# A graph network's node update moved from a stage of its own into the edge steps

## The reference

```python
x = x + gnn(layernorm(x), node_vec1, src, dst, edge_attr_4, edge_attr_8, ...)
x = x + ffn(layernorm(x), ...)
```

```python
hid = silu(edge_length_embedded @ fc_w0 / sqrt(8)); w = hid @ fc_w1 / 8
y0 = segment_sum(mid0, dst); y1 = segment_sum(mid1, dst)     # products of w, h[src] and the factors
out0 = c_s * s0 + c_x * (y0 @ W_lin2_0 * z / ...)            # s0, h0: x0 @ W_sc0, x0 @ W_lin1_0
```

## Time and profile before

| | us |
|---|---|
| median of three runs (lowest, highest) | 1195.45 (1194.55, 1196.22) |
| the profiled execution's own time | 1192.31 |
| its span in the trace | 1190.3 |
| first gather to last gather | 60.6 to 554.1 |
| first routed product to last add issued | 804.3 to 1184.2 |

### The profile page before, as it was taken

The page is one execution under the profiler, slowest core; times in us unless marked ns, Lnnn a source line. Parts: engine busy times, 40 slices in busy tenths (PEclk is TensorE's granted clock), DMA queues, the critical chain, the costliest instruction groups (busy, mean ns, idle before and its releaser), DMA issues. The chain is left out here.

```text
span 1190.3 us, 30949 instructions
## 1 busy us (share of the span) xinstructions
PE 1043.2 (88%) x8929; PEld 915.6 (77%) x8929; DVE 750.4 (63%) x1842; ACT 727.2 (61%) x2353; POOL 633.0 (53%) x645
## 2 busy tenths in 40 slices
PE   3788988889998988887688999988999999999991
PEld 2567777777777777776565999988999999899991
DVE  6566677766666667775476764445666656657561
ACT  3778888888888888886355645544444443444430
POOL 4077777777777777774000044442455455455552
PEclk9979999999999999999898999998999999999996
DMA  5233333343333433434554522323243444433221
GB/s 161 94 111 109 109 111 109 109 111 108 110 110 107 111 108 109 110 108 147 161 178 177 177 90 89 102 81 118 49 111 81 85 107 112 86 74 77 41 50 22
DMA packets 91911, 125.57 MB, mean 105 GB/s; under 512 B 29278, under 2 KB 70670, under 8 KB 91712
## 3 DMA queue, kind: packets, MB, share of 16 engines
q0 software_dynamic: 31792, 67.29, 22.9%
q1 hardware_dynamic: 56128, 54.01, 14.6%
q10 hardware_dynamic: 3920, 3.41, 0.8%
HBM read 98.30 MB, written 26.36 MB: 105 GB/s over the span
## 5 line engine op out<-in xcount | busy, mean ns | idle before, releaser
L568 ACT ACTIVATE hots<-hot,sh_st 128x64 f32<-128x64 f32 x1568 | 384.9, 334 | 0.2 <-issue 0.2
L711 PE MATMUL psY<-prod,hots 128*64 128x128 f32 x2352 | 279.4, 276 | 0.0
L707 PE MATMUL psY<-prod,hots 128*64 128x256 f32 x784 | 220.6, 401 | 52.1 <-DVE prod L615 52.1
L711 PEld LDWEIGHTS psY<-prod,hots 128*64 128x64 f32 x2352 | 256.0, 138 | 0.0
L543 POOL DMA_INDIRECT x_wlo<-h_tab,src_sb x224 | 214.2, 956 | 70.1 <-issue 70.1
L1738 ACT ACTIVATE q_hf<-q_psA,x_b 128x256 f32<-128x256 f32 x232 | 110.0, 474 | 191.9 <-PE q_psA L1282 186.5
L1683 POOL DMA_INDIRECT out_rows<-q_ob,q_index x58 | 119.9, 2068 | 136.1 <-DMA out_rows<-q_ob,q_index 89.2
L543 POOL DMA_INDIRECT rows<-h_tab,src_sb x168 | 161.0, 958 | 51.2 <-issue 51.2
L707 PEld LDWEIGHTS psY<-prod,hots 128*64 128x64 f32 x784 | 83.2, 136 | 91.0 <-DVE prod L615 89.4
L1282 PE MATMUL q_psA<-q_xhi,x_whi 128*128 x464 | 132.4, 285 | 9.4 <-DVE q_xlo L1776 9.0
L1869 PE MATMUL q_psB<-x_whi,q_hhi 128*128 128x256 f32 x464 | 133.0, 287 | 0.1
(11 more groups left out here) (212 smaller groups left out, 2281.2 us busy)
## 6 DMA issues: line engine op xcount, KB each, us to landing
x_raw<-in_w SPq DMA_DIRECT2D x18, 1024.0 KB, 5.8
x_wlo<-h_tab,src_sb POOLq DMA_INDIRECT x224
x_sb<-in_x SPq DMA_DIRECT2D x5, 640.0 KB, 5.4
h_tab<-x_sb ACTq DMA_DIRECT2D x5, 640.0 KB, 3.2
u_x<-in_x SPq DMA_DIRECT2D x5, 640.0 KB, 7.0
xnew_d<-u_x SPq DMA_DIRECT2D x5, 640.0 KB, 3.5
xn_d<-u_xn SPq DMA_DIRECT2D x5, 640.0 KB, 5.1
s_xnew<-xnew_d SPq DMA_DIRECT2D x5, 640.0 KB, 5.5
```

Of the source, the lines that this page charges most:

```text
L568: ins = nc.scalar.activation(hots[p][:, c, n, :], hot[p][:, c, :], ACT.Copy, scale=sh_st[p][:, 4 * c + n:4 * c + n + 1])
L707: nc.tensor.matmul(psY[p][0:SPAN, 0:FEAT], hots[p][:, c, 0, :], prod[p][:, c, 0:4, :].rearrange("p a u -> p (a u)"), start=(c == 0), stop= ...
L711: ins = nc.tensor.matmul(side[:, k::3 - k, :][:, 0:2, :], hots[p][:, c, k + 1, :], prod[p][:, c, 4::k + 1, :][:, 0:2, :], start=(c == 0 an ...
```

## The change

1. The gathers wait once a step, at gather 0, and only for the products that free their row buffer, and gather_turn is incremented once a step. There are four row buffers, all inside x_wlo.
2. update_block is gone. Its work on a pair of tiles is spread over the eight steps of an edge iteration: with k the iteration, the pair k-1 is turned and mixed and the pair k-2 is normed, turned, scored and stored. After the last step pairs 11 and the single tile 24 remain. psE and psW are single now, so radial(j) waits for the products of step j-1. The root is made on DVE by twelve chained steps on two columns (a guess by integer shift and three Newton steps) in place of ACT's square root. The scores come out as 128 x 8, so that they need no second turn.
3. The sums y and x + s are fetched by SP for each pair (fetch_y). x + s is added in node_block by POOL (base_of) and stored to HBM (base_d); h goes through a ring of its own. The spherical factors are loaded once, for all steps; the eight edge numbers are loaded for four steps at a time. A third condition is added to R: another pass if a step begins below the tiles that are already updated.
4. The shared expert's weights are loaded at the end of node_block, the high half is split by ACT in the edge steps, the low half by DVE after the last one. All five groups of columns go through HBM, and group 0 is loaded at the end of the edge block. xnew stays in the graph's order of columns, so that the shared part's add into ob is done in two instructions. The slot sends of POOL follow other points of the shared part.
5. In the routed part POOL issues the gather of a later tile between add(d, 0) and its landing, and waits for add(d, 1) to land right behind it. For the last expert, PE does all down products of the tile before first (apart), and DVE's output comes a tile sooner (early, late).

The core of the diff:

```diff
-    RING = 7
+    RING = 4
...
-        psE = [pb(f"psE{i}") for i in range(2)]
-        psW = [ctx.enter_context(nc.psum_tensor(f"psW{i}", [P, C, 4, MUL], F32)) for i in range(2)]
+        psE = pb("psE")
+        psW = ctx.enter_context(nc.psum_tensor("psW", [P, C, 4, MUL], F32))
...
                     for c in range(C):
                         if c == 0:
-                            pool.wait_ge(prod_done, (r * T + t) * 2 + 2)
-                        if c == 1 and t >= RING - 2:
-                            pool.wait_ge(hot_done, r * T + t - RING + 3)
-                        if c == 2:
-                            pool.wait_ge(prod_done, (r * T + t) * 2 + 3)
-                        pool.sem_inc(gather_turn, 1)
+                            pool.wait_ge(prod_done, (r * T + max(t, RING - 1)) * 2 + 2)
+                        if c == 0:
+                            pool.sem_inc(gather_turn, 1)
...
+            def base_of(g):
+                for j in range(GROUP):
+                    t = g * GROUP + j
+                    pool.wait_ge(s_ready, t + 1 + 2)
...
+                    pool.tensor_tensor(s_row[:, 0:MUL], s_row[:, 0:MUL], x_row[:, 0:MUL], ALU.add)
+                    pool.tensor_tensor(s_row[:, MUL:].rearrange("p (c u) -> p c u", c=3),
+                                       s_row[:, MUL:].rearrange("p (c u) -> p c u", c=3),
+                                       x_row[:, MUL:].rearrange("p (u c) -> p c u", c=3), ALU.add).then_inc(based, 1)
```

The order on PE, and DVE's programme of a step with the burst that the root belongs to:

```diff
+            def turn_of(r, k, q, done=None, at_work=None):        # PE
+                j = k * ITER + q
...
+                    hidden(r, k + (q + 2) // ITER, (q + 2) % ITER)
...
+                    radial(r, j + 1, (q + 1) % 2)
+                segment(r, j, q % 2)
+                if done is not None and q == 1:
+                    turn_x(r, done)
+                if done is not None and q == 3:
+                    score(r, done)
+                if at_work is not None and q == 3:
+                    pe.wait_ge(y_in, 32 * (r * IN_LOOP + at_work + 1))
+                    turn(r, at_work * PAIR, y_st[:, 0:2, :])
+                if at_work is not None and q == 5:
+                    pe.wait_ge(logits_out, r * (LAST + 1) + at_work + 1)
+                    mix(r, at_work * PAIR)
+                    turn(r, at_work * PAIR + 1, y_st[:, 2:4, :])
+                if at_work is not None and q == 7:
+                    mix(r, at_work * PAIR + 1)
...
+            def turn_of(r, k, q, done=None, at_work=None):        # DVE
...
+                    add_y(r, j - 2, q % 2)
...
+                    one_hot(r, j + 1, (q + 1) % 2)
+                if done is not None and q == 1:
+                    normalize(r, done)
+                products(r, k, j, q)
+                if done is not None and q == 0:
+                    graph_result(r, done, 1)
+                    variance(r, done)
+                if done is not None and q == 3:
+                    low(r, done)
+                if at_work is not None and q == 6:
+                    graph_result(r, at_work, 0)
```

What SP does for each iteration, and POOL's adds of the routed part:

```diff
+                with sp.Fori(2, ITERS - 1) as k:
+                    store_rows(r, k - 2)
+                    e_load(r, k * 2 + 2, 0)
+                    rows_stored(r, k - 2)
+                    fetch_y(r, k, k - 1)
+                    store_cols(r, k - 2)
+                    cols_stored(r, k - 2)
+                    e_load(r, k * 2 + 3, 1)
...
+                for p in range(ITERS - 2, LAST + 1):
+                    store_rows(r, p)
+                    rows_stored(r, p)
+                    store_cols(r, p)
+                    cols_stored(r, p)
...
             with pool.Fori(1, all_but_two) as d:
-                rows_of(within(d + 4, TILES + 1))
-                landed(d - 1, 1)
-                add(d, 0)
-                landed(d, 0)
-                add(d, 1)
+                adds(d, within(d + 4, TILES + 1))    # add 0, gather, landed 0, add 1, landed 1
```

More of the change, by code:

```diff
@@ new lines, in copy_logits, with split @@
+            def copy_logits(r, p):
+                n = parts(p)
+                act.wait_ge(scored, r * (LAST + 1) + p + 2)
+                first = act.snap(p * PAIR) if not isinstance(p, int) else p * PAIR
+                nc.scalar.activation(logits[:, at(first, n), :].rearrange("p t e -> p (t e)"),
+                                     psO[:, FEAT:FEAT + n * EXPERTS], ACT.Copy).then_inc(logits_out, 1)
+            def split(r, i):
+                part = slice(PIECE * i, PIECE * (i + 1))
+                nc.scalar.activation(whi0[:, part], raw[:, part], ACT.Copy).then_inc(whi_part, 1)
@@ L672, in _ @@
                 add_y(r, T - 2, 0)
                 add_y(r, T - 1, 1)
+                low(r, ITERS - 2)
+                dve.wait_ge(x_end_in, 16)
+                graph_result(r, ITERS - 1, 0)
+                graph_result(r, ITERS - 1, 1)
+                variance(r, ITERS - 1)
+                normalize(r, ITERS - 1)
+                graph_result(r, LAST, 0)
+                variance(r, LAST)
+                low(r, ITERS - 1)
+                normalize(r, LAST)
+                low(r, LAST)
@@ new lines, in _ @@
+            with pe.Fori(0, R) as r:
+                hidden(r, 0, 0)
+                hidden(r, 0, 1)
+                radial(r, 0, 0)
+                for q in range(ITER):
+                    turn_of(r, 0, q)
+                pe.wait_ge(w_ready, 1)
+                for q in range(ITER):
+                    turn_of(r, 1, q, None, 0)
+                with pe.Fori(2, ITERS) as k:
+                    for q in range(ITER):
+                        turn_of(r, k, q, k - 2, k - 1)
+                turn_of(r, ITERS, 0)
+                turn_of(r, ITERS, 1, ITERS - 2)
+                score(r, ITERS - 2)
+                pe.wait_ge(y_done, (r + 1) * T + 2)
+                pe.wait_ge(logits_out, r * (LAST + 1) + ITERS)
+                first = 2 * ITERS - 2
+                for t in range(first, NT):
+                    turn(r, t, y_sb[:, 2 * t:2 * t + 2, :])
+                    mix(r, t)
+                for p in range(ITERS - 1, LAST + 1):
+                    turn_x(r, p)
+                    score(r, p)
@@ L1803, in output, with tile @@
                                             None, ALU.mult).then_inc(ob_done, 1)
-            def tile(s, e, done=None, after=None):
+            def tile(s, e, done=None, after=None, early=None, late=None):
                 high(s, 0)
@@ L1813, in tile @@
                         output(*done)
+                    if f == 1 and early is not None:
+                        output(*early)
+                    if f == FC - 1 and late is not None:
+                        output(*late)
                     if f == 2:
@@ L1874, in down, with tile @@
                     ins.then_inc(down_done, 1)
-            def tile(s, e, done=None, fresh=False):
+            def tile(s, e, done=None, fresh=False, apart=False):
                 h = e % 2
@@ L1881, in tile @@
                     done_side = pe.snap(done[0] % 2)
+                if apart:
+                    for f in range(FC):
+                        down(*done, f, done_side)
                 for f in range(FC):
-                    if done is not None:
+                    if done is not None and not apart:
                         down(*done, f, done_side, fresh)
```

824 lines of the change are left out of this document (396 added, 428 removed).

## The result

The changed kernel takes 1257.41 us (median of 3, 1256.22 to 1259.74) against 1195.45: ratio 1.0522, 95% interval 1.0502 to 1.0543. It is 5% slower, 71 us above the forecast and 49 above the end of the range. The profiled execution took 1257.41 with a span of 1255.5, that of before 1192.31 with 1190.3, so the difference of the spans is 65.2.

| stretch | before | after | change | forecast |
|---|---|---|---|---|
| start to first gather | 60.6 | 70.3 | +9.7 | +3.5 |
| first gather to last sums added | 504.5 | 584.8 | +80.3 | +41 |
| from there to the shared expert | 91.7 | 39.8 | -51.9 | -56 |
| shared expert, to the routed part's first transposes | 147.5 | 145.2 | -2.3 | 0 |
| routed part to the end | 386.0 | 415.4 | +29.4 | +2 |

What follows compares the result with a forecast made beforehand. The prediction took POOL's gather line to bound the edge loop, with PE 0.59 us free per step. Its terms, +41 - 56 + 3.5 + 2 = -9.5, gave 1183 profiled, 1186 as median; range 1163 to 1208.

Steps and rivals of the forecast that it cites:

- Part 1: Edge gathers: one wait and increment per step, and a ring of four instead of seven, change the time by 0.
- Part 2: Update inside the edge steps: iterations take 44.2 us against 40.4, so the edge stage grows by 41 us (28 to 60).
- the upper bound: Edge iteration at most 46.1 us, with 0.17 us more issue at each of PE's eight update parts and normalize at 1.4.
- What is not hidden is one burst on DVE, because psW is now single: Edge steps: radial waits for all products of the step before, so PE stands 3.6 us once per iteration.
- Part 3: After the last edge, up to the shared expert: 35.7 us instead of 91.8, -56 (-51 to -60).
- Part 4: Node block: POOL's adds keep up, but the edge block waits for the last store: +3.5 us (+1 to +12).
- Part 5: Routed part: gather between add 0 and its landing, +0.6 and -0.5 us a round; sum +2 us (-3 to +25).
- Rival 3: Routed part: gathers beside DVE's casts are stretched as add 0 was, +23 us, 1209; chance 0.1.
- Add 0 lasts 2.0: Routed part: add 0's length of 2.0 us, used to put add 1 5.8 us after add 0 instead of 5.16.
- The sooner outputs gain nothing: Routed part, last expert: earlier outputs gain nothing, since DVE waits for POOL there already.
- Rival 2: Edge steps: burst and waits cost more, iterations over 45.1 us, slower from there; at 46.1 the time is 1205; chance 0.2.
- Rival 1: Edge steps: POOL stays the bound, iterations 40.4 to 42 us, edge stage grows 0 to 16, time 1153; chance 0.18.

Runs made afterwards that it cites:

- b_bufs: Kernel before with only the change's edge-loop buffers and waits (one gather wait and increment per step, psW and psE single), no update in the steps: 1198.11 us, 1.0021.
- e_fill: Changed kernel with six unread 512-column matmuls on PE ahead of the radial product that stands, once per iteration: 1239.08 us, 1.0372.
- e_wload: Changed kernel with the first expert's weight load (2 MB) moved from the node block's end to behind the edge block's first hidden product: 1255.95 us, 1.0505.
- e_index: Changed kernel with the two index copies of a tile's gather moved ahead of add 0, the gathers staying behind it: 1247.62 us, 1.0422.
- e_last: Changed kernel with only the last expert put back (outputs and downs as in other experts, adds in their new order): 1251.70 us, 1.0489.
- e_best: Changed kernel with DVE's burst cut up, routed part as before and weight load behind the first hidden product, in one: 1163.38 us, 0.9719.
- b_burst2: Kernel before, psW and psE double, with 28 chained two-column DVE steps (result unused) behind the products once in seven steps: 1238.34 us, 1.0356.

## Why the prediction was wrong, step by step

- **Part 1, gathers and ring: right.** 0 was forecast; b_bufs shows 2.5 us, with psW and psE single in the same run, so part 1 has at most that.
- **Part 2, the burst: place right, cause and size wrong.** The stand is where it was forecast, once per eight steps before radial until DVE's products. By its own times: result 1.12 us after products(8k) ended (forecast 1.3), last root step done after 5.3 (5.1), but then 1.23 us of "issue" before add_y, in which DVE computes nothing, normalize 1.23 in four pieces, and products(8k+1) done after 11.3 instead of 9.8. The stand is 5.3, not 3.6: the upper bound had held part of this (46.1 per iteration), and I chose the middle. The step "What is not hidden is one burst on DVE, because psW is now single" failed: in the kernel before, with a burst, PE stands with two psW as well, only 1 us less (5.0 and 6.0 us). The reason is in the kernel's order: segment(8k+1) needs the same late products, so a second psW is worth one product of PE's work.
- **The missing term: the clock.** The sum took PE's work at full speed after a stand, without a word on it. The runs show 2.5 us in each of ten iterations, 25 us. The kernel before has it too, once: after PE's first wait of 10.5 us its radial products last 2.08 us, as they do here. The Trainium skill (TensorE: Matmul & The Clock Gate, What's actually happening) has the clock follow how busy TensorE has lately been; here it fell within each stand of 5 us (in the one shown it is 1.00 until 314 and 0.50 from 315) and came back under work, and e_fill gives its price: 2.3 us an iteration with a filling 0.2 us too long.
  The edge stage missed its forecast by 39 us. Ten iterations at 47.7 instead of 44.2 are 35 of them: the stand +1.7, the clock +2.5, PE's own work 40.0 and not 40.6 (a pair costs 4.3 us and not 4.9). The other 4 lie in the first steps and in the last burst, ahead of segment(97).
- **Part 3, after the last edge: nearly right.** -52 for -56. PE runs these tiles at half clock (windows 655 to 695: 0.54): sixteen matmuls of a mix last 1.97 us against the 1.09 of the earlier trace rows. In e_fill, where they last 1.09, the stretch is 37.0 us instead of 39.8, so 2.8 of the 4 us missed are the clock's.
- **Part 4, the node block: a term left out.** POOL's add takes 0.33 + 0.67 = 1.0 us a tile (forecast 0.9, and 0.56 plus dispatch by the estimate beside it) and keeps up, and the border moved by 4.3 us (57.64 to 61.96) for 3.4 or so. But the shared expert's weights, 2 MB, also move from the end of the edge block into this border. Item 4 of the change names this load, and I did not cost it. e_wload gives it 3.6 us of the first gather's 9.7, and nothing of the total that can be told. The other 1.7 or so behind the border are not explained by a run.
- **Part 5, the routed part: wrong by 27.** The short rounds came out as forecast (add 0 to add 1 5.8 in the round that starts at 1006.86). The long ones, with DVE splitting weights, went from 6.4 to 8.2 and more. Two terms failed. "Add 0 lasts 2.0" was one round near the end, taken for all: in the kernel before it lasts 3.2 in ten of 29 rounds, and the mean from add 0 to add 1 is 5.54, not 5.16. And the index copies, 0.9 us under the old landing, take 2.1 to 2.7 beside the splits. Per round the forecast was +0.6 - 0.5; the runs show +1.1 - 0.2. Rival 3 had this place and nearly this price (+23), but that is luck in part: it named the gathers, whose mean grew by 0.04 us only (995 to 1032 ns) in the changed kernel. The rule cited for it, the Trainium skill, SBUF — State Buffer, Who interferes with whom, also says that a DVE instruction with two SBUF inputs contends with a GpSimd instruction that reads SBUF; the splits have two and the copies read one, so the rule bears on the copies, and the trace agrees (2.69 against 0.9). It does not let the gathers off: in e_index, where one starts in the copies' place, it lasts 1.98. The late rows for PE (23.8 us) stood nowhere in the prediction: it counted how long the gather takes where it now stands, and not who waits for its rows. "The sooner outputs gain nothing" held. That an early output can hold back DVE, and with it PE, for 6 us near the end was not in it; e_last shows 5.7 us for the last expert's edit.
- **Rivals.** Rival 2 (iterations over 45.1) was what happened to the edge stage, at 47.7 instead of its 46.1, and rival 3's cost came on top. Each was priced with the other parts at their forecast, and the range ended at 1208, though the two have nothing to do with each other: together they were 1186 + 19 + 23 = 1228, and the other 29 us are about what the clock took in the ten iterations and behind them. Rival 1 (1153) is what e_best comes near: with the burst cut up, iterations are 40.6.
- **Slips in the sums.** Twice the 2.52 us of the earlier trace rows is 5.0 for a pair, not 4.9; the upper bound's own terms give 45.9, not 46.1; 54.4 + 0.9 + 5 is 60.3, not 60.5; the chances add up to 0.99. None of them moves the forecast by more than 2 us.

## What to carry to other kernels

Work moved into a loop with free time is hidden only if each piece fits into one step's slack: here the same work took 66 us more in one burst than spread over seven steps. Where a stand of the matmul engine of some 5 us is forecast, add what the clock takes after it, here 2.5 us a time. And before a transfer or gather is put behind another operation, ask what that one waits for and who wants the rows, and give each moved DMA a price at its new place: here one that the change's description names had none.

## What was not expected of the hardware

- After a burst of small chained steps, DVE sits 1.23 us (0.91 in b_burst2) in "issue" before the next add, which first reads its row number into a register. The read itself takes 0.31 us of it (310.2 to 310.5); what the rest is, no run shows. In the edge steps of the kernel before, with the same read, the add never waits in "issue".
- Two index copies of 128x1 on POOL took from 0.31 us (e_index, ahead of the splits, beside DVE's output) through 0.9 to 2.69 beside DVE's weight splits. An indirect gather in their place took 1.98 instead of 0.95 to 1.0.
- The half clock lasted 5 us after each stand of 5.2 us. Filling the stand with unread matmuls removed it, and was worth 23 us in ten iterations.
